# Attention maxima for four heads: ScalarE writes all rows in one copy, VectorE's copy to three heads is removed

## The reference

```python
h = _layernorm(x, axis=-1) * (1 + ca) + sa
x = x + ga * _L0_attn_ref(h, L0_attn_w_qkv, L0_attn_b_qkv, L0_attn_w_out, L0_attn_b_out)
...
scores = jnp.einsum('bhqd,bhkd->bhqk', q, k) / math.sqrt(Hd)
causal = jnp.triu(jnp.full((S, S), -jnp.inf, dtype=scores.dtype), k=1)
scores = scores + causal[None, None]
attn = jax.nn.softmax(scores, axis=-1)
out = jnp.einsum('bhqk,bhkd->bhqd', attn, v)
...
h = _layernorm(x, axis=-1) * (1 + cb) + sb
x = x + gb * _L0_ffn_ref(h, L0_ffn_gate_weight, L0_ffn_wi, L0_ffn_wo)
```

## Time and profile before

| | |
|---|---|
| median of 3 runs | 786.88 us |
| the runs | 783.63, 786.88, 789.47 us |
| span of the profiled execution | 782.6 us |
| TensorE busy | 689.1 us, 88% |
| VectorE busy | 561.1 us, 72% |
| ScalarE busy | 459.5 us, 59% |
| mean granted TensorE clock | 0.943 of full |

### The profile page before, as it was taken

One profiled execution on the slowest core, in us unless ns is written; L12 is line 12 of the kernel. 1 busy time (PEld: TensorE's weight loads), 2 busy tenths in 40 slices (PEclk: granted clock), 3 DMA queues, 4 the chain that ended last, 5 costly groups with the idle time before them and its releaser, 6 DMA issues.

```text
span 782.6 us, 12208 instructions
## 1 busy us (share of the span) xinstructions
PE 689.1 (88%) x4290; PEld 367.2 (47%) x4290; DVE 561.1 (72%) x1467; ACT 459.5 (59%) x962; POOL 133.9 (17%) x194
## 2 busy tenths in 40 slices
PE   4686989999999998999999999989996279999994
PEld 3564534432323343323332323242543269999994
DVE  7754778788888787988888898960435437777762
ACT  1422445566676667766677676657783336656551
POOL 6000222220001132003310201100105300121122
PEclk9869889999999999999999999999999559999998
DMA  7436126630006033005900006000004283455200
GB/s 243 109 76 144 41 57 147 162 68 14 2 0 162 1 81 81 2 1 124 308 1 1 1 1 214 1 28 1 28 28 162 90 234 115 155 182 201 92 23 17
DMA packets 42111, 66.53 MB, mean 85 GB/s; under 512 B 3822, under 2 KB 31985, under 8 KB 41466
## 3 DMA queue, kind: packets, MB, share of 16 engines
q1 hardware_dynamic: 39746, 59.44, 27.3%
q0 software_dynamic: 2304, 6.31, 2.2%
HBM read 39.36 MB, written 26.78 MB: 85 GB/s over the span
## 4 chain that ended last, share of the span: by engine, by line
PE 74%; DVE 10%; ACT 8%; issue 4%; DMA 2%; POOL 1%; SPq 0%; DVEq 0%; POOLq 0%; ACTq 0%
PE bank L1245 17%; PE bank L1295 15%; PE bank L1325 14%; PE bank L1430 9%; PE bank L1413 8%; ACT probs L802 4%; PE bank L1187 3%; DVE chunk_max L1049 2%; PE bank L1350 2%; PE bank L1216 1%; PE bank L1396 1%; ACT qk_sb L751 1%; PE bank L1373 1%; PE bank L1228 1%; DVE stats L907 1%
## 5 line engine op out<-in xcount | busy, mean ns | idle before, releaser
L802 ACT ACTIVATE probs<-bank 128x512 f32<-128x512 f32 (+3 forms) x640 | 298.3, 537 | 124.1 <-PE bank L1325 123.0
L1049 DVE TENSOR_REDUCE chunk_max<-bank 128x1 f32<-128x512 f32 x384 | 250.7, 685 | 36.9 <-PE bank L1295 35.9
L1325 PE MATMUL bank<-stacks 104*128 104x512 bf16 (+3 forms) x640 | 195.4, 356 | 13.5 <-ACT probs L802 10.1
L1295 PE MATMUL bank<-stacks 96*128 96x512 bf16 (+3 forms) x640 | 197.7, 359 | 7.9 <-DVE chunk_max L1049 3.2
L1245 PE MATMUL bank<-probs,v_sb 128*32 128x512 f32 (+3 forms) x1280 | 151.6, 546 | 0.1
L1055 DVE CUSTOM_DVE_ANT_0 masked<-bank,causal 128x128 bf16<-128x128 f32 (+3 forms) x256 | 120.7, 484 | 15.4 <-PE bank L1295 14.6
L1295 PEld LDWEIGHTS bank<-stacks 96*128 96x128 bf16 x640 | 56.0, 98 | 160.0 <-DVE chunk_max L1049 79.4
L698 POOL TENSOR_SCALAR_AFFINE_SELECT probs<-probs 128x512 f32<-128x512 f32 x64 | 40.6, 635 | 397.4 <-ACT probs L802 397.4
L1325 PEld LDWEIGHTS bank<-stacks 104*128 104x128 bf16 x640 | 62.2, 100 | 98.7 <-ACT probs L802 65.6
L1430 PE MATMUL bank<-w_split,acts 128*128 128x256 f32 x576 | 79.9, 284 | 0.0
L1430 PEld LDWEIGHTS bank<-w_split,acts 128*128 128x128 f32 x576 | 74.5, 190 | 1.5 <-issue 0.8
(11 more groups left out here) (140 smaller groups left out, 533.6 us busy)
## 6 DMA issues: line engine op xcount, KB each, us to landing
stacks<-qk_rows SPq DMA_DIRECT2D x6, 1536.0 KB, 12.4
w_raw<-w_in SPq DMA_DIRECT2D x8, 1024.0 KB, 5.0
w_raw<-w_down SPq DMA_DIRECT2D x8, 1024.0 KB, 8.0
qk_rows<-part SPq DMA_DIRECT2D x32, 192.0 KB, 2.9
slot_rows<-empty SPq DMA_DIRECT2D x1, 5140.0 KB, 28.9
slots_sb<-slot_rows SPq DMA_DIRECT2D x8, 514.0 KB, 4.0
qk_rows<-part SPq DMA_DIRECT2D x32, 128.0 KB, 2.4
stacks<-qk_rows SPq DMA_DIRECT2D x8, 384.0 KB, 4.5
```

The source lines that it names most:

```text
L802: act.activation(probs[:, s % 3, h, 0:width], bank[SCORE_BANKS[u % 3]][:, 0:width], ACT.Exp)\
L1049: dve.tensor_reduce(to, src[:, 0:QB], AX.X, ALU.max).then_inc(max_read, 1)
L1295: pe.matmul(bank[MAX_BANKS[u % 3]][:, 0:width], stack(g, 0)[0:KR, h, q0:q0 + P], stack(g, 1)[0:KR, h, c * QB:c * QB + width], start=True, ...
L1325: pe.matmul(bank[SCORE_BANKS[u % 3]][:, 0:QB - lo], stack(g, 1)[0:KR + MR, h, kt * P:(kt + 1) * P], stack(g, 0)[0:KR + MR, h, b * QB + lo: ...
```

## The change

ScalarE's copy of the transposed maxima writes all four heads in one instruction. Its source is the same 8 x 512 region of bank 7, read four times over (a dimension with stride 0), and its destination has the four heads' 512 columns, 2048 elements on each of 8 partitions. The one-element copy, VectorE's copy and their two semaphores are gone. The block's first score matmul waits for the count of ScalarE's reads of bank 7 instead. Since the same count tells that the bank is free, bank 7's next user also waits for the whole copy.

```diff
@@ scalar
                     act.wait_ge(misc_done, misc_use[ev] + 1)
-                    act.copy(stack(g, 0)[KR:KR + MR, 0, b * QB:(b + 1) * QB],
-                             bank[MISC_BANK][:, :].bitcast(BF16)[0:MR, 0:QB]).then_inc(misc_read_a, 1)
-                    act.wait_ge(misc_read_a, misc_reads(misc_use[ev])[0] + 1)
-                    act.copy(c_tmp[0:1, 1, 0:1], c_tmp[0:1, 0, 0:1]).then_inc(max_row0, 1)
+                    act.copy(stack(g, 0)[KR:KR + MR, :, b * QB:(b + 1) * QB],
+                             bank[MISC_BANK][:, :].bitcast(BF16)[0:MR, 0:QB].rearrange("m (h s) -> m h s", h=1)
+                             .broadcast_to([MR, HG, QB])).then_inc(misc_read_a, 1)
@@ vector
-                if ev[0] == "max_rows":
-
-                    n = ev[1]
-                    g, b = divmod(n, NB)
-                    rows = stack(g, 0)[KR:KR + MR, :, b * QB:(b + 1) * QB]
-                    dve.wait_ge(max_row0, n + 1)
-                    dve.tensor_copy(rows[:, 1:HG, :], rows[:, 0:1, :].broadcast_to([MR, HG - 1, QB]))\
-                        .then_inc(max_rows, 1)
@@ tensor
                     if kt == key_tiles(b)[0] and h == 0:
-                        pe.wait_ge(max_rows, n + 1)
+                        pe.wait_ge(misc_read_a, misc_reads(misc_use["max_rows", n])[0] + 1)
```

More of the change, by code:

```diff
@@ L436, in layer @@
         max_parts = sem("max_parts")
-        max_row0 = sem("max_row0")
-        max_rows = sem("max_rows")
         scored = sem("scored")
```

## The result

The changed kernel takes 794.31 us (median of 12 runs), the kernel before 786.4 in the 12 runs beside them: ratio 1.0102, 95% interval 1.0077 to 1.0127, that is 8.0 us slower (6.1 to 10.0). The forecast was 792.5, 5.7 us slower. The ratio leaves out one run of each kernel that took over 1.5% more than its fastest (796.26 us before, 803.40 after).

A forecast was written before the change was run, and what follows sets the result against it. The prediction saw a ring of three engines with three PSUM banks per loop, TensorE having the most work. Terms 5.1 + 1.3 - 1.1 + 0.4 = +5.7 us took 786.88 to 792.5; forecast 789 to 795, 8 in 10 range 783 to 799.

The forecast's parts named there:

- The hold: At each block's row copy, ScalarE is held 1.06 us longer before the next exponential, 17.0 us in all.
- The six blocks of the first kind: Blocks 5, 7, 8, 11, 14, 15: copy stands ahead of a step's first exponential, fourth score waits; net +5.1 us.
- VectorE's head start: In five of blocks 5, 7, 8, 11, 14, 15, shorter waits for maxima give back 0.25 us each, 1.3 us.
- Block 6: The transpose of the heads needs the bank that the copy reads and goes 1.29 us later; +1.3 us.
- The rival on the clock: Block 6's standstill grows from 1.3 to 2.6 us, TensorE's clock falls; one to three stretches give 794 to 798; chance 0.13.
- Blocks 0 to 3: TensorE goes for the rows at once; rows 0.34 us later, but maxima no longer find VectorE late; -1.1 us.
- The clear gain of block 2: VectorE's copy stands ahead of a maximum whose bank TensorE waits for; all of its 0.69 us goes.
- Blocks 4, 9, 10, 12, 13: The copy follows exponentials of its step, with up to a step of room in the ring; +0.4 us.
- The sign on the clock: The forecast is wrong if the clock differs between the traces by more than one short stretch.
- VectorE sets the pace: Rival: ScalarE's longer hold goes into its idle time, each block gives back 0.69 us; 11 us faster, 776; chance 0.12.
- the ring absorbs it: Rival: the 1.06 us delay becomes fewer waits for maxima in the steps behind; time 787; chance 0.22.
- every block pays in full: Rival: blocks counted as hidden also lose 1.06 us, 17.2 us in sum; 804; chance 0.08.

The follow-up runs named there:

- e1: One-copy form only in blocks 5, 6, 7, 8, 11, 14 and 15, the others as in the kernel before; 1.0112, 8.8 us slower than before.
- e3: The kernel before with two more ScalarE copies to scratch in each block, holding ScalarE about 1.2 us longer; 1.0099, 7.8 us slower than before.
- e10: One-copy form only in blocks 5, 7, 8, 11 and 14, the others as in the kernel before; 1.0084, 6.6 us slower than before.
- e2: One-copy form only in blocks 0 to 4, 9, 10, 12 and 13, the others as in the kernel before; 0.9985, 1.2 us faster.
- e5: The kernel before without VectorE's copies, score matmuls of heads 1 to 3 taking 96 rows instead of 104; 0.9901, 7.8 us faster than before.

## Why the prediction was right, by its steps

*The price of the copy.* 1.86 us forecast, 1.852 measured in all 16.

*The hold.* 1.06 us a block forecast, 1.18 measured (1.88 against 0.70 between the copy's start and the next exponential's). I took off an overlap of 0.1 us that this copy doesn't have. Over five blocks that pay it in full or nearly so, it makes 0.6 us.

*The six blocks of the first kind, +5.1.* The mechanism is shown by e1, e3 and e10. Blocks 5, 7, 8, 11 and 14 lose 5.4 us, where 4.3 of the 5.1 were meant for them. For block 15 the step failed: 0.8 us was forecast and nothing is lost. In e1, whose stretch of low clock in this block is as long as that of the kernel before, the shift grows by 0.01 us; in the change it rises by 1.2 us at the copy and is back to 0.1 within two steps. The 0.25 us a block that I took back from VectorE's head start came in block 14 (0.5) and hardly elsewhere (5: 0.1; 8 and 11: 0).

*Block 6, +1.3.* Right as a stop (2.84 against 1.55 us from start to start), and only the late release of the bank makes it (e3: nothing). The rival on the clock has this standstill at 1.3 us before; the row says 1.17, and it grew to 2.45. The stretch of low clock behind it wasn't in the sum; it was a rival with 0.13. In the profile it brings the block to 2.9.

*Blocks 0 to 3, -1.1.* Not shown. The clear gain of block 2 is there at first: its next exponential starts 1.0 to 1.2 us earlier relative to the row copy, in e2 and in the change. In e2 it is given back within two to three steps. These blocks sum to -0.8 us in e2 and to +0.8 in the change's own profile, but kernels that change nothing there show -1.3 to 1.4. Of e2's -0.8 nearly all falls in block 0 (-0.7), where e10 has -0.7 unchanged. So what is left of the gain is about nothing.

*Blocks 4, 9, 10, 12, 13, +0.4.* Measured +1.1 in both profiles that have it: 0.1, 0.3, 0.7, 0.3, -0.3. The order of their sizes was right.

*The sum.* +5.7 forecast, 8.0 measured. With the measured terms, nothing for blocks 0 to 3 and no clock it is 5.4 + 1.3 + 1.1 = 7.8, and the estimate at one clock is 7.5. So the mechanism, ScalarE's hold at five places and the bank at block 6, is shown; the terms were too low by 1.1 us (hold and VectorE's giving back), 0.7 (blocks 4, 9, 10, 12, 13) and 1.1 (blocks 0 to 3), and too high by 0.8 in block 15. That the sum came within 2.3 us is in part luck, since these don't all point one way.

*The sign on the clock.* The forecast called itself wrong if the clock differed between the traces by more than one short stretch. It does: three stretches behind blocks 6, 7 and 11 that the kernel before lacks, and none at 526 us, where it has one. The sign was badly chosen, since the same kernel's clock varies as much from run to run (0.932 to 0.946 among the 70 runs before), and the times came out near the sum all the same.

*The rivals.* That VectorE sets the pace, 776 us, is refuted by the result itself and bounded by e5 (2.7 us where the change could gain). That the ring absorbs it is refuted by e10 for those five blocks, though it did come true in block 15. That every block pays in full is refuted by e2. The clock's part is plain in the profiles; in the runs the estimate has it at 0.9 us, which can't be told from nothing.

## What to carry to other kernels

When engines work in a ring with few buffers, what costs is a long hold at a place where the next engine has one buffer left, not the sum of work: 2.4 us a block in four pieces was free, 1.85 us in one was not. Ask of a merged instruction what stands behind it on its engine and who waits for that, and whether it holds a buffer longer; here the busier engine on average was the wrong one to relieve. An engine's idle time read at one step is no promise for the next; look at the very places where the work will stand.

## What the runs showed of the hardware

A copy of 8 partitions from PSUM on ScalarE let the next exponential start only at its end (0.60 us after the start of the 0.57 us copy, 1.88 after that of the 1.85 us one), while exponentials follow each other at 0.48 us with 0.60 us each. A standstill of TensorE of 2.4 us and more in block 6 (2.44 to 2.94) was followed by a stretch at low clock in four profiles of four, one of 1.17 us in none of eight; one of 2.3 us at another place in eight of twelve. In the kernel before, a mean granted clock lower by 0.001 went with 0.66 us more. Two GpSimd clears of 8 x 6144 bf16 elements, 5.38 and 5.25 us, stopped two of VectorE's `tensor_scalar` instructions (128 x 256 f32) for as long. And the start of the attention, ahead of which nothing is changed, varies by up to 4.7 us from profile to profile.
